# Edge MLP of a graph network on one core: eight pairs of gathered rows in place of four, and the landing signal moved ahead of the slot wait

## What is computed

```
msg_in   = concat(x[row], x[col], edge_features)      # 53125 x (128+128+64)
h        = relu(msg_in @ W1.T + b1)
messages = h @ W2.T + b2
agg      = segment_sum(messages, col, 3125)
g        = relu(concat(x, agg) @ U1.T + c1)
x        = layernorm(x + g @ U2.T + c2)
```

## Time and profile before

| what | before |
|---|---|
| device time, 3 runs | 2331.29 us median, 2327.55 to 2335.05 |
| profiled execution, span | 2761.6 us, 430 us (18%) above the median |
| profiled execution, time beside the span | none is given: the span, first to last instruction, is its time |
| first to last gather of the edge MLP, profiled | 617.9 to 1353.0 us, 735.1 us |
| first to last gather of the interaction, profiled | 2000.0 to 2703.0 us, 703.0 us |
| 416 gathers of the edge MLP | 0.944 us each on GpSimd (median), one every 1.25 us when nothing holds them |

### The profile page before, as it was taken

The page is one execution under the profiler, slowest core; times in us unless marked ns, Lnnn a source line. Parts: engine busy times, 40 slices in busy tenths (PEclk is TensorE's granted clock), DMA queues, the critical chain, the costliest instruction groups (busy, mean ns, idle before and its releaser), DMA issues. The chain is left out here.

```text
span 2761.6 us, 42960 instructions
## 1 busy us (share of the span) xinstructions
PE 1939.0 (70%) x8321; PEld 1389.5 (50%) x8321; DVE 1549.5 (56%) x4666; ACT 912.1 (33%) x2111; POOL 1358.6 (49%) x1337
## 2 busy tenths in 40 slices
PE   4886787776666666666779989899845555555557
PEld 3664455455566565656554544445633444444345
DVE  7997911144455455555355667556645556565555
ACT  3994111111111111111144062350334444444443
POOL 0001277715555555555327757487165555555550
PEclk9997988875555555555579999999866666676667
DMA  0001011122333333333311111111321112111111
GB/s 10 0 0 37 1 19 18 17 61 81 82 84 84 80 85 85 84 84 83 84 30 18 19 12 18 14 17 19 126 52 45 47 48 50 47 50 48 48 46 32
DMA packets 195712, 128.60 MB, mean 47 GB/s; under 512 B 138368, under 2 KB 177985, under 8 KB 194614
## 3 DMA queue, kind: packets, MB, share of 16 engines
q0 software_dynamic: 40256, 60.21, 10.1%
q1 hardware_dynamic: 151415, 58.11, 8.6%
q10 hardware_dynamic: 3841, 8.16, 0.9%
HBM read 106.83 MB, written 13.34 MB: 44 GB/s over the span
## 5 line engine op out<-in xcount | busy, mean ns | idle before, releaser
L1202 POOL DMA_INDIRECT work<-p_rows,small x416 | 395.9, 952 | 340.3 <-DVE work L1279 197.8
L2134 POOL DMA_INDIRECT adj<-h_rows,adj x416 | 395.1, 950 | 337.2 <-DVE adj L2219 189.8
L2351 PE MATMUL ps<-adj 128*128 128x125 f32 x928 | 224.8, 385 | 319.7 <-DVE adj L2229 220.6
L2351 PEld LDWEIGHTS ps<-adj 128*128 128x128 f32 x928 | 194.1, 281 | 406.4 <-issue 372.5
L1561 POOL DMA_INDIRECT edge_rows<-pay,small x289 | 351.0, 1214 | 88.4 <-issue 87.2
L1369 PE MATMUL ps<-work 128*128 x1024 | 300.3, 448 | 123.0 <-DVE work L1260 95.1
L1380 PE MATMUL ps<-small,work 128*128 128x64 f32 x1024 | 249.8, 399 | 152.4 <-issue 152.2
L1380 PEld LDWEIGHTS ps<-small,work 128*128 128x128 f32 x1024 | 242.0, 325 | 168.3 <-issue 168.0
L1321 ACT ACTIVATE work<-work 128x256 f32<-128x256 f32 x256 | 106.6, 416 | 656.9 <-DVE work L1279 432.9
L1369 PEld LDWEIGHTS ps<-work 128*128 128x128 f32 x1024 | 236.6, 320 | 139.2 <-issue 135.4
L1923 PE MATMUL ps<-adj,extra 125*128 (+2 forms) x1092 | 224.4, 352 | 8.9 <-issue 7.3
(11 more groups left out here) (388 smaller groups left out, 3156.1 us busy)
## 6 DMA issues: line engine op xcount, KB each, us to landing
work<-dst_all SPq DMA_DIRECT2D x256, 64.0 KB
work<-edge_attr SPq DMA_DIRECT2D x256, 64.0 KB
edge_rows<-pay,small POOLq DMA_INDIRECT x425
work<-p_rows,small POOLq DMA_INDIRECT x416
adj<-h_rows,adj POOLq DMA_INDIRECT x416
adj<-adj SPq DMA_DIRECT2D x232, 24.0 KB
pay<-edge_pay SPq DMA_DIRECT2D x106, 46.9 KB
adj<-edge_rows ACTq DMA_DIRECT2D x1, 2496.0 KB
```

Source lines behind the costliest of these rows:

```text
L1202: eng.indirect_dma_start(gathered[:, at:at + D], None, p_rows[:, :], bass.IndirectOffsetOnAxis(ap=src_i[:, c:c + 1], axis=0)).then_inc(s_g ...
L2134: eng.indirect_dma_start(gathered[:, at:at + D], None, h_rows[:, :], bass.IndirectOffsetOnAxis(ap=row3_i[:, c, DST_C:DST_C + 1], axis=0)). ...
L2351: ins = eng.matmul(SUM[v % 2], msg[b][:, k * D:(k + 1) * D], hot[b][:, k * P:(k + 1) * P], start=k == 0, stop=k == PAIR - 1)
```

## The change

`RING` goes from 4 to 8. The buffer `gathered`, now 128 x 2048 float32, is all of `extra` and no longer part of `work`. In GpSimd's loop the wait for the landing of pair g - 2, with the signal behind it, stands ahead of the wait for pair g's slot and of pair g's two gathers. The number of instructions changes by four slot waits (pairs 4 to 7 have none any more); there are eight landing semaphores in place of four.

```
-KB, RING, LAG = 3, 4, 2
+KB, RING, LAG = 3, 8, 2
...
-    gathered, dst_f = l_(EW, RING * PAIR * D), l_(EW, PAIR * PAIRS)
+    gathered, dst_f = G["extra"][0:EW, 0:RING * PAIR * D], l_(EW, PAIR * PAIRS)
...
             for g in range(PAIRS + LAG):
+                if g >= LAG:
+                    eng.wait_ge(s_g[(g - LAG) % RING], 16 * PAIR * ((g - LAG) // RING + 1))
+                    eng.nop(nofuse=True).then_inc(s_gd, 1)
                 if g < PAIRS:
                     if g >= RING:
                         n = eng.value_load(done[0:1, g - RING:g - RING + 1], min_val=1, max_val=VISITS)
...
                         eng.indirect_dma_start(gathered[:, at:at + D], None, p_rows[:, :],
                                                bass.IndirectOffsetOnAxis(ap=src_i[:, c:c + 1], axis=0)
                                                ).then_inc(s_g[g % RING], 16)
-                if g >= LAG:
-                    eng.wait_ge(s_g[(g - LAG) % RING], 16 * PAIR * ((g - LAG) // RING + 1))
-                    eng.nop(nofuse=True).then_inc(s_gd, 1)
```

## The result

| | before | changed |
|---|---|---|
| device time, median | 2329.6 us, 4 runs, 2327.55 to 2335.05 | 2392.33 us, 4 runs, 2389.95 to 2395.18 |
| ratio | | 1.0271, 95% interval 1.0257 to 1.0285: slower |
| span of the profiled execution | 2761.6 us (first), 2326.8 us (second, below) | 2388.2 us |

The change costs 62.7 us. The side was forecast (slower, 0.50), the size was not: 20 us forecast, 2392.3 outside the range of 2308 to 2366.

What follows compares the result with a forecast made beforehand. The prediction took GpSimd's gather issue to bound the edge loop in timed runs. Slots, signal and the other engines counted 0 us and the landing wait 20 us: 2331 + 20 = 2351 us, range 2308 to 2366.

Steps and rivals of the forecast that it cites:

- What bounds the loop: Edge MLP's loop: in timed executions GpSimd's gather issue bounds it, 2.50 us a pair, about 520 us.
- More slots: Edge MLP's gather ring: four more slots and the buffer's new place remove 0 us, since four slots suffice.
- The signal: GpSimd's landing signal in the edge MLP's loop: already goes out as soon as the rows have landed; 0 us saved.
- The landing wait ahead of the gathers: GpSimd's edge MLP loop: waiting for pair g - 2 before pair g's gathers costs 26 us, taken as 20; chance 0.50.
- The chain: GpSimd, second gather of pair g - 2 through landing, signal and slot wait to pair g's first: 4.0 us against 3.75.
- The upper bound, 36 us: Edge MLP's loop: the landing wait's cost if a landing takes 0.1 us more now and then.
- Hidden after all: Edge MLP's loop: landing to gather under 3.75 us, or VectorE and TensorE the bound; no change, 2331 us; chance 0.34.
- Faster, by the slots: Edge MLP's loop: some stalls occur in timed runs and extra slots let GpSimd gather through them; 2306 us at largest; chance 0.16.
- The idle time stands before each pair's first gather: Changed kernel's profile, GpSimd: in stretches without a slot wait, idle time would stand before each pair's first gather.
- Two pairs in 5.1 to 5.3 us: Changed kernel's profile, stretches without a slot wait: two pairs of gathers take this in place of 5.0 us.
- Waits named for a landing up from 0.9 to tens of us: Changed kernel's profile: GpSimd's waits on a landing, 0.9 us before, would rise to tens of us.
- Slot waits under 60 us: Changed kernel's profile: GpSimd's slot waits, 197.8 us before, fall under 60 us or move to where stalls fill eight slots.

Runs made afterwards that it cites:

- the second profile: The kernel before, unchanged, profiled once more: 2328.5 us, span 2326.8 us, edge MLP's gather loop 520.8 us.
- experiment 9: Against the kernel before: one gather for each pair in place of two, the second column's rows left at zero; 2275.91 us, ratio 0.9749.
- experiment 2: Against the kernel before: eight slots in the buffer extra, landing wait left where it was; 2328.17 us, ratio 0.9997.
- experiment 3: Against the kernel before: only the order changed, landing wait ahead of the slot wait, with four slots in work; 2396.84 us, ratio 1.0282.
- experiment 10: Against the changed kernel: each edge-feature load brings 16 of 256 columns; 2850.48 us, ratio 1.0006 to the kernel before, 2850.01 us on that chip.
- experiment 6: Against the changed kernel: done is read ahead of the landing wait; 2358.27 us, ratio 1.0117 to the kernel before.
- experiment 5: Against the changed kernel: the wait ahead of pair g is for the landing of pair g - 1; 2911.61 us, ratio 1.2499 to the kernel before.

## Why the prediction was right in kind and wrong in size

**What bounds the loop: right.** The profile at hand showed VectorE and stalls as the bound. Setting it aside because it was 430 us over the timed runs, and putting both gather loops at GpSimd's pace, gave 520 us; the second profile has 520.8 and 521.4 us, and experiment 9 shows that taking gathers away shortens the edge MLP's.

**More slots: right at 0** (experiment 2). **The signal: right at 0**: in the second profile of before it already goes out 0.48 us (mean) after the pair's last packet, in the changed kernel 0.45 us after.

**The landing wait ahead of the gathers: right mechanism, wrong size.** This is the term that failed: 20 us were taken for it, and the loop grew by 61.4 us. It failed in three steps.
- The chain was put at 2.6 + 0.7 + 0.7 = 4.0 us. The loop of the changed kernel gives what the chain came to: 582.2 / 207 = 2.81 us a pair, 5.62 us for two, less 1.25 us: 4.37 us. 0.37 us more for two pairs is 0.185 us a pair, 38 us. Link by link, worked out from the trace: second gather to last packet 2.37 us mean over all pairs (2.28 median, 2.12 to 2.85 for the middle 90%) and last packet to signal 0.45, so 2.83 us where 2.6 was taken; signal to slot wait 0.66 us where 0.7 was taken; slot wait to gather, over the 114 pairs whose gather started late, 0.81 us (0.72 mostly, 1.8 in nine of them) where 0.7 was taken. The 2.6 came from pairs 1 and 3 of the first profile, with last packets at 2.25 and 2.22 us where that profile's own mean is 2.32, and the 0.7 of the last link from a single gather. Near-best cases were added up as if they were means.
- The means come to 4.3 us, and the rest of the 4.37 is the spread of the landings: a late one is lost, and an early one isn't won back, since GpSimd can't gather faster than its pace. An estimate from the trace shows its size. Taken through the loop pair by pair with the 208 measured landings, 0.66 and 0.81 us for the other two links and 1.255 us for a gather, the loop comes to 582 us, as measured; with the mean landing for every pair it comes to 574. The recorded sum has 10 us for this in its upper bound alone, and nothing in its 26.
- Of the 26 us that even so came out, 20 were taken, because the steps came from an execution 18% too long and might shrink. They did not: a gather lasts 0.944 us (median) in both profiles of before, and its landing takes 2.48 us in the second against 2.32 us in the first; only the stalls between the steps were gone. 26 + 38 is 64 us, against 62.7 measured and 61.4 in the loop.

The upper bound, 36 us, failed by the same step: it allowed 0.1 us for late landings, where links and spread together were 0.37 us above the chain.

**The rivals.** "Hidden after all" is out by experiment 3. It rested on a landing of 1.9 us, that of a direct DMA. The trace has 2.37 us to the last packet and 2.83 to the signal, so the row of the gathers themselves was the one to go by. By the Trainium skill, "DMA: Bandwidth & Descriptors", section "Anatomy of one DMA — SWDGE (gpsimd) path", such a gather takes about 2.0 us and its 64 KB at 436 GB/s, an estimate of 2.15 us. The changed kernel's trace doesn't agree: its earliest signal comes 2.43 us after the second gather. That rival's other half, VectorE and the stalls as the bound, may occur on experiment 10's chip. "Faster, by the slots" is out by experiment 2, on the chips that run the kernel before in about 2330 us.

**Two readings that don't hold**, though the sum doesn't rest on them. In the earlier trace rows GpSimd's gathers at 1017.10 and 1018.35 start inside VectorE's idle time (1016.35 to 1020.76) and not ahead of it, and the three engines are idle at the same time for 2.8 us (1017.98 to 1020.76), not for 4 to 5; they start again within 1.45 us of each other. And two figures have no working: the 8 us of the landing wait's lower end, and the 25 us of the rival "faster", whose working comes to 34.

**What the profile should have shown.** The idle time stands before each pair's first gather: right. Two pairs in 5.1 to 5.3 us: 5.62. Waits named for a landing up from 0.9 to tens of us: 18.9 us stand there, but they are 62 pieces of at most 0.3 us, the plain time between two gathers; the real landing waits go by VectorE's name or by "issue". Slot waits under 60 us: the view says 76.2, and none of them is a wait for a slot. A span within 20 us of 2761.6: wrong, the profile of the changed kernel was of an execution without the stalls, 2388.2 us.

## What to carry to other kernels

A wait in an instruction stream costs what it keeps waiting behind it: count from the event waited for to the start of the next piece of work through every instruction between, with means and not best cases, and compare with the time that the pace leaves between these two points. Here a chain of 4.37 us cost 2.7% of the kernel where 3.75 us were left for it, and nothing where 6.25 us were. Where chain and time are close, the spread counts as well. Put a wait for one's own transfers behind the issue of the next ones, or wait for an older one, and read what the wait doesn't need before it. Before summing on a profile compare its span with the timed runs, and if they don't agree, take single durations from it and not its bound.

## What was not expected of the hardware

- The same program took about 2330 us on four chips and 2850 us on a fifth, in all 13 timed runs there. In the trace taken on the fifth, TensorE, VectorE and ScalarE are idle together for more than 2 us 31 times in the edge MLP's loop; in the first profile of before it is 44 times, about every 14 us, and in the second not once. GpSimd goes on starting gathers in these stalls (46 of them in the first profile). What makes them is open.
- A loop with a landing in its chain loses by the spread of the landings as well as by their mean. In experiment 6 the links' means (2.45 + 0.47 + 0.10 + 0.8 to 0.9, some 3.9 us) are only 0.1 to 0.2 us over the 3.75 us allowed, and the loop lost 0.14 us a pair, as much as a steady 4.03 us would. The same estimate as above, with this run's landings and 0.8 us for the last link, gives 548 us against 549.7 measured; with their mean in place of each, 527.
- A slot wait long satisfied can be named as the releaser for an engine's idle time: 589.8 us of it in experiment 5, where the add had ended over 30 us before.
